# Four-layer cross-attention: softmax weights of layer 1 and inputs of layer 3 transposed by 32x32 squares and transfers, layer-3 query product in plain float32, token rows updated in place

## What is computed

```python
def attend(x, key, Wq, bq, Wk, bk, Wv, bv):          # per batch
    Q, K, V = x @ Wq + bq, key @ Wk + bk, key @ Wv + bv
    return softmax(Q @ K.T * 256**-0.5) @ V

x = x + attend(x, ctx, L0...) @ Wo + bo                            # layer 0
o = sum(attend(ln(x), ln(k), ...) @ Wo + bo for k in (ctx, side))  # layer 1, LayerNorms with gains
x = x + o
x = x + ln(x) @ fc_W + fc_b                                        # fc
x = ln(x + softmax_over_tokens(x @ Wq @ (ctx @ Wk).T) @ (ctx @ Wv)) * gamma + beta   # layer 2
x = x + attend(x, ctx, L3...) @ Wo + bo                            # layer 3
```

## Time and profile before

| | |
|---|---|
| runs of the kernel | 557.55, 557.83, 558.46 us (median 557.83) |
| profiled execution, first to last instruction (its span; the profile gives no other time for it) | 557.1 us |
| TensorE (PE) busy | 545.8 us, 98% |
| weight loads on TensorE (PEld) busy | 534.9 us, 96% |
| GpSimd (POOL) busy | 480.7 us, 86% |
| VectorE (DVE) busy | 478.4 us, 86% |
| ScalarE (ACT) busy | 447.2 us, 80% |
| moved by DMA | 76.58 MB, 137 GB/s |

### The profile page before, as it was taken

How to read it: one execution, slowest core, us unless ns; L and a number is a source line. 1 busy time by engine, 2 the same in 40 slices (tenths; PEclk the granted TensorE clock), 3 DMA queues, 4 the chain that set the end, 5 groups by cost and what they waited for, 6 DMA issues and landing times.

```text
span 557.1 us, 16210 instructions
## 1 busy us (share of the span) xinstructions
PE 545.8 (98%) x4492; PEld 534.9 (96%) x4492; DVE 478.4 (86%) x1472; ACT 447.2 (80%) x1568; POOL 480.7 (86%) x672
## 2 busy tenths in 40 slices
PE   8999999999999999999999999999999999999995
PEld 7999999999999999989999999999999999999994
DVE  2588799888999889989897997999898987998884
ACT  2799987889778797869879798877888979798663
POOL 4999997999988989979997899977999998766793
PEclk9999999999999999999999999999999999999999
DMA  8993472344553345453247263453433432221112
GB/s 238 352 326 126 118 215 90 121 147 149 172 168 111 113 143 152 149 174 124 80 139 202 67 190 102 145 172 122 139 122 115 124 105 78 77 96 58 39 40 95
DMA packets 74440, 76.58 MB, mean 137 GB/s; under 512 B 7664, under 2 KB 58224, under 8 KB 74352
## 3 DMA queue, kind: packets, MB, share of 16 engines
q1 hardware_dynamic: 74352, 75.55, 43.0%
HBM read 50.87 MB, written 24.64 MB: 136 GB/s over the span
## 4 chain that ended last, share of the span: by engine, by line
PE 87%; POOL 4%; DMA 3%; issue 2%; DVE 2%; SPq 1%; ACT 1%; DVEq 0%; POOLq 0%; ACTq 0%
PE bank L793 15%; PE bank L806 10%; PE bank L800 9%; PE bank L776 7%; PE bank L817 5%; PE bank L819 5%; PE bank L818 5%; PE bank L949 5%; PE bank L927 5%; PE bank L784 5%; PE bank L830 4%; PE bank L902 3%; PE bank L903 3%; PE bank L904 3%; DMA side_in<-in_side 1%
## 5 line engine op out<-in xcount | busy, mean ns | idle before, releaser
L1065 ACT ACTIVATE prob_L<-bank,neg_max_L 128x128 f32<-128x128 f32 x320 | 114.5, 375 | 15.7 <-DVE neg_max_L L1376 13.6
L1065 ACT ACTIVATION_READ_ACCUMULATOR prob_L<-bank,neg_max_L 128x1 f32 x320 | 68.3, 214 | 0.0
L1376 DVE TENSOR_REDUCE neg_max_L<-bank 128x2 f32<-128x256 f32 (+1 forms) x128 | 60.5, 479 | 7.1 <-PE bank L800 4.3
L1546 POOL TENSOR_TENSOR rstd_ln<-var_eps_ln,minus_half 128x2 f32<-128x2 f32 x64 | 45.2, 707 | 18.5 <-ACT var_eps_ln L1078 18.2
L994 ACT ACTIVATE oT_hi_L<-bank 128x256 fp32r<-128x256 f32 (+1 forms) x96 | 44.4, 471 | 12.4 <-PE bank L806 11.1
L1219 DVE TENSOR_TENSOR oT_lo_L<-bank,oT_hi_L 128x256 fp32r<-128x256 f32 (+1 forms) x96 | 47.2, 501 | 5.6 <-ACT oT_hi_L L994 4.9
L994 ACT ACTIVATE probT_L<-bank 128x256 f32<-128x256 f32 (+1 forms) x96 | 44.4, 470 | 9.0 <-PE bank L784 8.6
L1333 DVE BATCH_NORM_STATS2 stats_ln<-x 128x6 f32<-128x256 f32 x128 | 47.5, 413 | 0.2
L1219 DVE TENSOR_TENSOR xT_lo_L<-bank,xT_hi_L 128x512 fp32r<-128x512 f32 x64 | 43.1, 677 | 3.7 <-ACT xT_hi_L L994 3.5
L1611 POOL TENSOR_TENSOR x_bias<-x,bias_fc 128x512 f32<-128x512 f32 x32 | 41.1, 1285 | 5.8 <-DVE x L1409 5.8
L1588 POOL TENSOR_TENSOR xT_lo_L<-x_in,xT_hi_L 128x512 fp32r<-128x512 f32 x32 | 41.2, 1286 | 5.4 <-ACT xT_hi_L L994 5.4
(11 more groups left out here) (228 smaller groups left out, 2294.2 us busy)
## 6 DMA issues: line engine op xcount, KB each, us to landing
x_in<-in_x SPq DMA_DIRECT2D x32, 512.0 KB, 3.8
ctx_in<-in_ctx SPq DMA_DIRECT2D x32, 256.0 KB, 2.8
keys_out<-keys_turned SPq DMA_DIRECT2D x32, 256.0 KB, 2.2
keysT<-keys_out SPq DMA_DIRECT2D x128, 64.0 KB, 2.0
out<-y SPq DMA_DIRECT2D x32, 256.0 KB, 2.3
x_out<-x_turned SPq DMA_DIRECT2D x30, 256.0 KB, 2.2
x3T<-x_out SPq DMA_DIRECT2D x120, 64.0 KB, 2.3
side_in<-in_side SPq DMA_DIRECT2D x32, 128.0 KB, 2.7
```

The source lines that it names most:

```text
L1065: last = activation(at(prob[k], g)[:, b, :], block(bank, b), ACT.Exp, bias=at(neg_max[k], g)[:, b:b + 1], accum_out=at(total[k], g)[:, b:b ...
L1376: dve.tensor_reduce(at(neg_max[k], g)[:], scores, AX.X, ALU.max, negate=True).then_inc(done[f"max_{k}"], 1)
L1546: pool.tensor_tensor(at(rstd[k], g)[:], at(var_eps[k], g)[:], minus_half[:, 0:n], ALU.pow).then_inc(done[f"rstd_{k}"], 1)
```

## The change

1. **`prob_L1`** (softmax weights of layer 1), groups 0 to 29: `PT_L1` on TensorE and its eviction `pT_L1` on ScalarE go. VectorE turns the squares (`turn_prob`), SP sends and fetches (`send_prob`, `fetch_prob`), and `O_L1` reads the fetched tile. Groups 30 and 31 keep the old way.
2. **`x5`** (layer 3's input rows): the same with `turn_x5`, `send_x5`, `fetch_x5` in place of `T_L3` and its eviction.
3. **`Q_L3`**: no hi and lo parts; two plain float32 matmuls per batch of the whole M (`M_L3`) with the fetched rows, in place of six fp32r passes over both batches. VectorE's `lo_L3` goes for all 32 groups, ScalarE's `hi_L3` for 30.
4. **Token rows in place**: one ring `x` of 12 tiles is loaded, gets its biases and products in place, is normalised in place and stored. The transposed input comes by a transfer of its own (`load_xT`). The bias steps wait for the readers of the tile: `x1_bias` for `norm_ln1`, `x2_bias` for `T_fc` and `stats_lnf`, `x_gamma` for `turn_x5`; `out_L2` waits for `turn_x3`. The freed room goes to second buffers (`xT_hi_L1`, `qT_L1`, `probT_L1`, `prob_L2` and others).
5. **A new order** of every engine's list (`STARTS`, `PREPARATIONS`, `SEATS` have new numbers throughout), the loads at the start included.

```diff
+LATE_ONLY = ("PT_L1", "pT_L1", "T_L2", "hi_L2", "T_L3", "hi_L3")
+IN_FLIGHT = 4
-    "keys_turned": 1, "x3_turned": 1, "x3T": 2, "less_mean_ln2": 2}
+    "rstd_ln2": 2, "ctxT_hi": 2, "ctxT_lo": 1, "shift_ln2": 2, "V2": 3, "keys_turned": 2, "x3_turned": 2, "x3T": 3,
+    "less_mean_ln2": 2, "xhat": 2, "x": 12, "xT_in": 3, "x5_turned": 1, "x5T": 2, "prob_turned": 1}
...
             def load_x(g):
-                earlier(sp, "x_bias", g, len(x_in))
-                earlier(sp, "lo_L0", g, len(x_in))
-                sp.dma_start(at(x_in, g)[:].rearrange("p a n -> p (a n)"), ins["x"][g]).then_inc(at(landed["x"], g), 16)
+                earlier(sp, "x_bias", g, IN_FLIGHT)
+                if g >= len(x):
+                    before = g - len(x)
+                    sp.wait_ge(at(stored, before), 16 * (before // IN_FLIGHT + 1))
+                sp.dma_start(flat(at(x, g)), ins["x"][g, :, 0:GROUP * D]).then_inc(at(x_landed, g), 16)
+
+            def load_xT(g):
+                earlier(sp, "lo_L0", g, len(xT_in))
+                sp.dma_start(at(xT_in, g)[:], ins["x"][g, :, GROUP * D:]).then_inc(at(landed["xT"], g), 16)
...
+            def send_x5(g):
+                sp.wait_ge(done["turn_x5"], g + 1)
+                sp.dma_start(x5_out[g], at(x5_turned, g)[:]).then_inc(at(x5_sent, g), 16)
+
+            def fetch_x5(g):
+                sp.wait_ge(at(x5_sent, g), 16 * (g // len(x5_turned) + 1))
+                earlier(sp, "Q_L3", g, len(x5T))
+                exchanged(at(x5T, g), x5_out[g], at(x5_back, g))
...
             def O_L1(g):
-                pe.wait_ge(done["pT_L1"], g + 1)
-                attended("L1", g, at(keys, g))
+                if g < LATE:
+                    pe.wait_ge(at(prob_back, g), 16 * (P // SQUARE) * (g // len(probT["L1"]) + 1))
+                else:
+                    pe.wait_ge(done["pT_L1"], g - LATE + 1)
+                bank = bank_for(pe, "O_L1", g)
+                pT = squares(at(probT["L1"], g))
+                for b in range(A["L1"] * GROUP):
+                    last = mm(block(bank, b), at(keys, g)[:, b, :], pT[:, b], start=True, stop=True)
+                last.then_inc(done["O_L1"], 1)
...
             def Q_L3(g):
-                pe.wait_ge(done["lo_L3"], g + 1)
-                if g == 0:
-                    prepared(pe, "M_lo_L3")
-                queries("L3", g)
+                if g == 0:
+                    prepared(pe, "M_all_L3")
+                if g < LATE:
+                    pe.wait_ge(at(x5_back, g), 16 * (P // SQUARE) * (g // len(x5T) + 1))
+                else:
+                    pe.wait_ge(done["hi_L3"], g - LATE + 1)
+                bank = bank_for(pe, "Q_L3", g)
+                xT = squares(at(x5T, g))
+                for b in range(GROUP):
+                    for t in range(T):
+                        last = mm(block(bank, b), M_L3[:, t, :], xT[:, b * T + t], start=t == 0, stop=t == T - 1)
+                last.then_inc(done["Q_L3"], 1)
...
+            def turn_prob(g):
+                dve.wait_ge(done["prob_L1"], g + 1)
+                if g >= len(prob_turned):
+                    dve.wait_ge(at(prob_sent, g), 16 * (g // len(prob_turned)))
+                dve.transpose(squares(at(prob_turned, g)), in_blocks(flat(at(prob["L1"], g)))).then_inc(done["turn_prob"], 1)
...
             def x1_bias_of(g):
                 if g == 0:
                     prepared(pool, "bias_L1")
-                pool.wait_ge(done["out_L0"], g + 1)
-                earlier(pool, "out_L1", g, len(x1_bias))
-                pool.tensor_tensor(at(x1_bias, g)[:], at(x1, g)[:], every(bias["L1"]), ALU.add).then_inc(done["x1_bias"], 1)
+                pool.wait_ge(done["norm_ln1"], g + 1)
+                pool.tensor_tensor(at(x, g)[:], at(x, g)[:], every(bias["L1"]), ALU.add).then_inc(done["x1_bias"], 1)
```

More of the change, by code:

```diff
@@ L634, in fetch_keys, with send_prob, fetch_prob @@
                 exchanged(at(keysT, g), keys_out[g], at(keys_back, g))
+            def send_prob(g):
+                sp.wait_ge(done["turn_prob"], g + 1)
+                sp.dma_start(prob_out[g], at(prob_turned, g)[:]).then_inc(at(prob_sent, g), 16)
+            def fetch_prob(g):
+                sp.wait_ge(at(prob_sent, g), 16 * (g // len(prob_turned) + 1))
+                earlier(sp, "O_L1", g, len(probT["L1"]))
+                exchanged(at(probT["L1"], g), prob_out[g], at(prob_back, g))
             def send_x3(g):
@@ L1133, in hi_L2, with hi_L3 @@
                 copied(squares(at(x3T, g)), in_blocks(bank_of("T_L2", g)[:]), "hi_L2")
+            def hi_L3(g):
+                act.wait_ge(done["T_L3"], g - LATE + 1)
+                earlier(act, "Q_L3", g, len(x5T))
+                copied(squares(at(x5T, g)), in_blocks(bank_of("T_L3", g)[:]), "hi_L3")
             def exp_L0(g):
@@ L1142, in exp_L1 @@
                 act.wait_ge(done["max_L1"], g + 1)
-                earlier(act, "PT_L1", g, len(prob["L1"]))
+                if g >= len(prob["L1"]):
+                    late = g - len(prob["L1"]) - LATE
+                    if late < 0:
+                        act.wait_ge(done["turn_prob"], g - len(prob["L1"]) + 1)
+                    else:
+                        act.wait_ge(done["PT_L1"], late + 1)
                 earlier(act, "inv_L1", g, len(total["L1"]))
@@ L1421, in out_L1 @@
                 dve.wait_ge(done["OUT_L1"], g + 1)
-                earlier(dve, "x2_bias", g, len(x2))
-                earlier(dve, "T_fc", g, len(x2))
-                plus("out_L1", g, "OUT_L1", x1_bias, x2)
+                plus("out_L1", g, "OUT_L1")
             def out_fc(g):
@@ L1429, in out_fc @@
                 dve.wait_ge(done["OUT_fc"], g + 1)
-                earlier(dve, "turn_x3", g, len(x3))
-                earlier(dve, "out_L2", g, len(x3))
-                scaled_plus("out_fc", g, "OUT_fc", rstd["lnf"], x2_bias, x3)
+                scaled_plus("out_fc", g, "OUT_fc", rstd["lnf"])
             def v_L2(g):
@@ L1608, in x2_bias_of @@
                     prepared(pool, "bias_fc")
[L1609 to L1611 removed]
+                pool.wait_ge(done["T_fc"], g + 1)
+                pool.wait_ge(done["stats_lnf"], g + 1)
+                pool.tensor_tensor(at(x, g)[:], at(x, g)[:], every(bias["fc"]), ALU.add).then_inc(done["x2_bias"], 1)
             def prob_L2(g):
```

307 lines of the change are left out of this document (157 added, 150 removed), and 431 rows, old and new, of tables (COPIES, EMPTIED_BY, PREPARATIONS, SEATS).

## The result

The changed kernel takes **595.4 us** (median of 4 runs, 593.68 to 599.1) against 558.1 us for the kernel before, measured beside it: ratio 1.066, 95% interval 1.059 to 1.073. I had forecast 545.1 us with a range of 536 to 556. It went the other way, by 37 us, and 39 us above the upper end. The profiled execution took 594.8 us, its span is 592.9 us.

What follows compares the result with a forecast made beforehand. TensorE's full queue was taken as the bound. From 557.1 us of span, -26.4 (transposes) + 5.7 (float32 query) + 4 (exchanges) + 4 (start) gave 544.4, or 545.1 us as run median; range 536 to 556.

Steps and rivals of the forecast that it cites:

- TensorE, -26.4 + 5.7 us: On TensorE, 240 fewer transpose records save 26.4 us; the float32 query product costs 5.7; busy time becomes 525.1 us.
- VectorE, +20.3 us, covered: On VectorE, 60 added turns minus lo_L3 raise work from 478.4 to 498.7 us, hidden if kept 92% busy.
- The 578 us rival: VectorE becomes the bound and keeps all its idle time, slower than before: 578 us, chance 0.06.
- The prices that I set beside the rule of the Trainium skill: At 0.70 us on VectorE against 0.44 on TensorE, 60 moved tiles would cost 15.6 us instead of saving 26.4.
- ScalarE and GpSimd, nothing: ScalarE loses 36.7 us of evictions beside TensorE's work; GpSimd keeps 480.7 us with new waits; both priced at nothing.
- The exchanges, +4 us, bounds 0 and 18: TensorE's waits for 90 fetched tiles (prob, x3, x5): 4 us taken, from 0.05 us each; upper bound 0.2 us each.
- The sum of 6.7 us for an exchange: One tile's way: turn 0.70, send to landing 2.2, three fetches issued 1.5, last fetch to landing 2.3 us.
- the cover of 7.6 to 8.6: Median TensorE work on other groups hiding an exchange: 7.6 us for x3, 8.6 for prob, 8.5 for x5.
- The transfers themselves have room: On the transfer engines, 60 more exchanges add 31.5 MB, taking the mean share from 43.0% to 61%.
- The start, +4 us: WkT_L0 lands at 17.6 us or a little later instead of 13.7, delaying TensorE's layer 0; bounds 0 and 6.
- The exchanges are late: Rival: late fetches hold back sends on SP, 0.15 us for each of 90 exchanges, 13.5 us: 554.6 us, chance 0.20.
- What would show it: Listed signs, among them TensorE's waits for probT, x3T, x5T: 4 to 6 us expected, over 10 meaning late exchanges.

Runs made afterwards that it cites:

- no_sends: Changed kernel with all four exchanges fetching the input x instead of sent data, without landing waits, and their 122 sends removed; result incomplete: 550.2 us, ratio 0.985.
- start_order: Changed kernel with only the first loads reordered: layer 2's weights first, x of groups 0 to 3 later; 597.9 us, ratio 1.071.
- weights_first: Changed kernel with x of groups 1 to 3 and the key exchanges of groups 0 to 2 put behind weights in SyncE's list; 594.9 us.

## Why the prediction was wrong, point by point

- **TensorE, -26.4 + 5.7 us: right in the records, not in the busy time.** 4316 records, and where nothing else is late, as in `no_sends`, they go at 0.119 us each. Busy time was to be 525.1 us and is 539.7; the stretches at 1.2 GHz are some 9 us of that, by the estimate above.
- **VectorE, +20.3 us, covered: right in kind.** It grew by 14.1 us to 492.5 us (forecast 499), and with the transfers' load off it runs at 98% of a stretch without being waited for. The 578 us rival did not happen. The prices that I set beside the rule of the Trainium skill (VectorE: DVE Perf Modes, Rules for kernel authors) would have put the sum 42 us higher, at 587 us, nearer to the result than mine; but that would have been luck, as the reason is another: the turns are the same in the run of 550 us.
- **ScalarE and GpSimd, nothing: not contradicted.** GpSimd has its 480.8 us; ScalarE fell by 28.9 us to 418.3, not by 36.7, and TensorE hardly waits for either, in the changed kernel or in `no_sends`. But the chain of `no_sends` is GpSimd for 22%, so its 63 us of slack are less room than they look.
- **The exchanges, +4 us, bounds 0 and 18: this is the step that failed.** By the swap with TensorE's transposes the two added exchanges cost 39 us, at the forecast worth of the transposes; their landing waits and sends alone are 27 us (595.4 - 568.5), those of all four 45 us (595.4 - 550.2). The sum of 6.7 us for an exchange had no time for a finished tile to stand in SyncE's list: that was 1.0 to 1.4 us, and the way became 8.7 to 9.4 us, longer than the cover of 7.6 to 8.6. I had the load on SyncE right, 11.6 of 17 us a group, and took the rest as room, because the sum was under 17. I priced one exchange by what TensorE had waited for `x3T` when the list had gaps, and wrote the blocking ("everything behind such a wait waits too") down without pricing it. I also counted it too low: beside the 26.4 us of the earlier trace rows the list stood 16.1 us for `keys_out`, and these 42.5 us became 94.3. The average still does not fill the list (issues and landing waits are some 425 of 593 us); what it lacks is room at the moment when a tile is ready. The bound of 18 us was a fraction picked from one wait, not a sum over the list. The estimated 9 us of slow clock behind such pauses had no term at all.
- **"The transfers themselves have room": half wrong.** At 58 to 60% mean share nothing is full, yet landings lengthen (2.2 to 2.4 us for `x_out`, 2.2 to 2.7 for `keys_out`), and 1 MB more a group in 4 issues cost the kernel before 21 us.
- **The start, +4 us: mechanism right, term mis-sized.** This is the second term that failed. `WkT_L0` was to land at 17.6 us or a little later; it landed at 17.5 and its product began at 17.64. But I looked at that one product. TensorE's first product of all waited for 9.1 us, and by 200 us 135 records were missing even without the exchanges: 16 us where I had 4. How much of it would come back in the changed kernel is not shown, since `start_order` made the start worse (186 records by 50 us against 225) and `weights_first` hardly better (232).
- **The rivals.** "The exchanges are late" had the cause and 554.6 us; its 0.15 us for each of 90 exchanges is 0.31 by TensorE's own waits (27.6 us) and far more by what it set off. What would show it was well chosen: over 10 us of waits for the three tiles named the cause at once. I gave "slower" 0.06, all of it to VectorE. No case of mine ended slower by way of SyncE; it should have been there, since the list's 25 transfers and its blocking waits were both in the text.

## What to carry to other kernels

An in-order list of transfers is an engine: add up its issues **and** the landings that it stands for, per group, against the time of a group, and ask what is queued behind each wait. Work moved from the bound to such a list pays only while the list has gaps: here the first exchange about paid for itself and the second lost some 20 us. An average under the time of a group is not enough; ask how long a finished tile stands before its send. To price a chain through several resources, load the old kernel with the new traffic first: the dummy exchanges cost 54 us, which gives the sign and roughly the size (39 us in the changed kernel) without touching the order of any engine but SyncE.

## What the runs showed that I had not expected

- Issuing is not free of the shape: a transfer of 4 bytes took SyncE a median of 0.25 us in a row of four and 0.29 alone, a fetch of 64 KB in 512-byte runs a median of 0.43 us, and single ones up to 2.7 us:

```profile
L655 SPq DMA_DIRECT2D x5T<-x_out x120: 302/432/2698, 115.4 to 571.9; - x120
```

- Unused traffic of 1 MB a group, with the transfer engines at 60% and hardly a wait added, slowed a kernel whose bound was TensorE by 4%.
- A pause of 3.9 us on TensorE in the first 15 us can cost the gain of an earlier start: the granted clock of 0.65 and 0.83 in the two stretches of 10 us there is 5 us of TensorE's time, an estimate, where the first product had begun 4.5 us earlier.
- The same holds in the middle of the program: TensorE's clock was at 1.2 GHz for some 7 us after a wait of 2.7 us for one fetched tile.
